# Expert-choice words of a cross-attention and mixture-of-experts kernel: turned by VectorE in squares of 32 and sent by four DMAs, so that the row comes back by column

## The reference, cut to what matters

```
x = x + xattn(layernorm(x), ctx)                       # 16 heads of 8
t = rmsnorm(layernorm(x)) * norm_w                     # [tokens, 128]
topw, topi = top_k(softmax(t @ gate_w.T), 2)           # 2 of 8 experts
h1 = t @ w1.T + 2 * (t @ a1[e].T) @ b1[e].T            # per chosen expert e, 512 wide
h3 = t @ w3.T + 2 * (t @ a3[e].T) @ b3[e].T
act = silu(h1) * h3
out = sum over the two e of weight_e * (act @ w2.T + 2 * (act @ a2[e].T) @ b2[e].T)
x = x + out
```

## Time and profile before

| | |
|---|---|
| time, median of 3 runs | 298.48 us (297.51 to 298.67) |
| time of the profiled execution | 297.54 us, span 295.8 us |
| TensorE busy | 285.6 us, 97% of the span |
| VectorE busy | 224.1 us, 76% |
| ScalarE busy | 187.6 us, 63% |
| GpSimd busy | 180.8 us, 61% |
| granted TensorE clock | 0.999 |
| DMA | 12.45 MB, mean 42 GB/s |

### The profile page before, as it was taken

One profiled execution on the slowest core, in us unless ns is written; L12 is line 12 of the kernel. 1 busy time (PEld: TensorE's weight loads), 2 busy tenths in 40 slices (PEclk: granted clock), 3 DMA queues, 4 the chain that ended last, 5 costly groups with the idle time before them and its releaser, 6 DMA issues. The chain is left out here.

```text
span 295.8 us, 4543 instructions
## 1 busy us (share of the span) xinstructions
PE 285.6 (97%) x1499; PEld 238.0 (80%) x1499; DVE 224.1 (76%) x610; ACT 187.6 (63%) x310; POOL 180.8 (61%) x183
## 2 busy tenths in 40 slices
PE   8779999999999999999999999999999999999995
PEld 6547788878888888888888888888888887878884
DVE  3878996986689658894589765895579965795694
ACT  2478967674945966757855868459656658555542
POOL 3376599198970889429990589608982389518400
PEclk9999999999999999999999999999999999999999
DMA  5720020100210021200221011200012000100001
GB/s 155 281 72 3 0 73 1 72 3 25 81 71 2 0 72 38 71 1 2 71 71 39 0 53 55 71 0 2 1 37 73 0 0 35 75 1 0 35 2 35
DMA packets 7225, 12.45 MB, mean 42 GB/s; under 512 B 1825, under 2 KB 3234, under 8 KB 7202
## 3 DMA queue, kind: packets, MB, share of 16 engines
q1 hardware_dynamic: 6768, 11.77, 11.5%
q10 hardware_dynamic: 434, 0.39, 0.4%
HBM read 10.03 MB, written 2.13 MB: 41 GB/s over the span
## 5 line engine op out<-in xcount | busy, mean ns | idle before, releaser
L1010 ACT ACTIVATE silu<-h_ps 128x512 f32<-128x512 f32 x64 | 37.5, 597 | 33.2 <-PE h_ps L642 31.7
L1681 POOL TENSOR_TENSOR um_lo<-umf,um_hi 128x1024 fp32r<-128x1024 f32 x7 | 16.9, 2409 | 60.4 <-ACT um_hi L1002 60.4
L642 PE MATMUL h_ps<-um_hi,b_hi 128*128 128x512 f32 x128 | 51.4, 401 | 0.0
L642 PE MATMUL h_ps<-um_lo,b_hi 128*128 128x512 f32 x128 | 50.3, 393 | 0.6 <-DVE um_lo L1330 0.6
L642 PE MATMUL h_ps<-um_hi,b_lo 128*128 128x512 f32 x128 | 49.9, 390 | 0.0
L1343 DVE TENSOR_TENSOR act_second<-silu,h_ps 128x512 f32<-128x512 f32 x32 | 21.7, 680 | 17.2 <-PE h_ps L642 15.3
L1343 DVE TENSOR_TENSOR act_first<-silu,h_ps 128x512 f32<-128x512 f32 x32 | 21.4, 680 | 15.9 <-ACT silu L1010 12.7
L1703 POOL TENSOR_TENSOR scaled<-act_second,ratio 128x512 f32<-128x512 f32 x23 | 29.8, 1297 | 1.3 <-DVE act_second L1343 1.3
L642 PEld LDWEIGHTS h_ps<-um_lo,b_hi 128*128 128x128 f32 x128 | 24.0, 188 | 7.1 <-DVE um_lo L1330 1.4
L1002 ACT CAST um_hi<-umf 128x1024 fp32r<-128x1024 f32 x14 | 14.8, 1054 | 23.2 <-DVE umf L1324 22.2
L642 PEld LDWEIGHTS h_ps<-um_hi,b_lo 128*128 128x128 f32 x128 | 24.1, 188 | 4.5
(11 more groups left out here) (294 smaller groups left out, 793.0 us busy)
## 6 DMA issues: line engine op xcount, KB each, us to landing
chosen<-choice_dram SPq DMA_DIRECT2D x7, 512.0 KB, 3.5
x_in<-in_x_dram SPq DMA_DIRECT2D x7, 256.0 KB, 2.9
ctx_in<-in_ctx_t_dram SPq DMA_DIRECT2D x7, 256.0 KB, 3.2
out_dram<-y SPq DMA_DIRECT2D x7, 256.0 KB, 2.0
act_second<-in_hidden_w_dram SPq DMA_DIRECT2D x1, 512.0 KB, 4.3
act_second<-in_lora_w_dram SPq DMA_DIRECT2D x1, 512.0 KB, 5.4
v_parts<-in_down_w_dram SPq DMA_DIRECT2D x1, 512.0 KB, 4.8
ctx_in<-in_ctx_t_dram ACTq DMA_DIRECT2D x2, 128.0 KB, 3.2
```

What stands on the lines that cost most here:

```text
L642: mm = nc.tensor.matmul((h1_ps, h3_ps)[s][n % 2][:], b13[w][:, s, c * P:(c + 1) * P], um[k][m][:, s, :], start=False, stop=(i == 2), skip_ ...
L1010: nc.scalar.activation(silu[:, n % SILU_RING, :], h1_ps[n % 2][:], ACT.Silu).then_inc(silu_done.sem, 1)
L1681: nc.gpsimd.tensor_tensor(um[1][1][:], umf[1][:], as_f32(um[1][0][:]), ALU.subtract)\
```

## The change

`choice` grows to 32 words for each token, of which eight are used; GpSimd clears it once at the start. A new VectorE instruction (`turn_choice`, one transpose of 128x32 in four squares of 32x32) turns it into `choice_t`, where partition 32a + c holds word c of the tokens 32a to 32a + 31. It stands in VectorE's program between `act_step(b, 5)` and `act_step(b, 6)` of every block but the last. SyncE then waits for this instruction and no longer for GpSimd's, and sends four DMAs of 8 partitions x 32 words in place of one of 128 partitions x 8 words. The row in DRAM and in `chosen` now runs over all tokens for word 0, then for word 1, and so on. The indices of the two choices now share a word, so the masks read bf16 elements 4 bytes apart and `ratio` reads its float32 elements next to each other. A pad of 8 words in SBUF is gone.

```diff
-        choice = sb("choice", [P, CHOICE])
-        chosen = sb("chosen", [P, P * CHOICE])
-
-        sb("spacer", [P, 8])
+        choice = sb("choice", [P, SQUARE])
+        choice_t = sb("choice_t", [P, SQUARE])
+        chosen = sb("chosen", [P, CHOICE * P])
...
         def chosen_index(k):
-            words = chosen[:].bitcast(BF16).rearrange("q (p c) -> q c p", c=2 * CHOICE)
-            return words[:, k * TILES:(k + 1) * TILES, :]
+            words = chosen[:].bitcast(BF16).rearrange("q (c p k) -> q c p k", c=CHOICE, k=TOP)
+            return words[:, 0:TILES, :, k]
 
         def chosen_gap():
-            return chosen[:].rearrange("q (p c) -> q c p", c=CHOICE)[:, INDICES // 2:, :]
+            return chosen[:, INDICES // 2 * P:]
...
             def spread_choice(n):
-                sp.wait_ge(choice_done.sem, choice_done.of(n))
-                sp.dma_start(choice_dram[n % 2].rearrange("(p c) -> p c", c=CHOICE), choice[:])\
-                    .then_inc(choice_out.sem, 16)
+                sp.wait_ge(choice_turned.sem, choice_turned.of(n))
+                rows_out = choice_dram[n % 2].rearrange("(c a p) -> a c p", c=CHOICE, p=SQUARE)
+                for a in range(P // SQUARE):
+                    sp.dma_start(rows_out[a], choice_t[a * SQUARE:a * SQUARE + CHOICE, :]).then_inc(choice_out.sem, 16)
                 sp.wait_ge(choice_out.sem, choice_out.of(n))
...
+            def turn_choice(n):
+                ve.wait_ge(choice_done.sem, choice_done.of(n))
+                if n > 1:
+                    ve.wait_ge(choice_out.sem, choice_out.of(n - 1))
+                nc.vector.transpose(choice_t[:], choice[:]).then_inc(choice_turned.sem, 1)
+
...
             act_step(0, 5)
+            turn_choice(1)
             first_weight(0)
             act_step(0, 6)
...
                 act_step(b, 5)
+                turn_choice(b + 1)
                 act_step(b, 6)
```

More of the change, by code:

```diff
@@ L45 @@
 CHOICE = INDICES // 2 + TILES
+SQUARE = 32
 WKV, A13, W13, B13, W2A2, B2 = range(6)
@@ L166, in build_program @@
         gap = sb("gap", [P, TILES])
-        choice = sb("choice", [P, CHOICE])
-        chosen = sb("chosen", [P, P * CHOICE])
-        sb("spacer", [P, 8])
-        choice_index, choice_gap = choice[:, 0:INDICES // 2].bitcast(BF16), choice[:, INDICES // 2:]
+        choice = sb("choice", [P, SQUARE])
+        choice_t = sb("choice_t", [P, SQUARE])
+        chosen = sb("chosen", [P, CHOICE * P])
+        choice_index, choice_gap = choice[:, 0:INDICES // 2].bitcast(BF16), choice[:, INDICES // 2:CHOICE]
         row_expert_sb = sb("row_expert_sb", [P, 1])
@@ L321, in build_program @@
         row_expert_in = sem("row_expert_in")
+        choice_clear = sem("choice_clear")
         choice_done = signal("choice_done", first=0)
-        choice_out = signal("choice_out", 16, first=0)
+        choice_turned = signal("choice_turned", first=0)
+        choice_out = signal("choice_out", 16 * (P // SQUARE), first=0)
         chosen_in = signal("chosen_in", 16, first=0)
@@ L997, in exp_ratio @@
                 sc.wait_ge(mask_scaled.sem, mask_scaled.of(n - 1))
-                nc.scalar.activation(tile4(ratio), chosen_gap(), ACT.Exp).then_inc(ratio_done.sem, 1)
+                nc.scalar.activation(ratio[:], chosen_gap(), ACT.Exp).then_inc(ratio_done.sem, 1)
             def um_high(n, k):
@@ L1669, in choice_words @@
                 pool.wait_ge(top_i_done.sem, top_i_done.of(n))
-                if n > 1:
-                    pool.wait_ge(choice_out.sem, choice_out.of(n - 1))
+                if n == 1:
+                    pool.wait_ge(choice_clear, 1)
+                else:
+                    pool.wait_ge(choice_turned.sem, choice_turned.of(n - 1))
                     pool.wait_ge(e_gap_done.sem, e_gap_done.of(n - 1))
@@ L1675, in choice_words @@
                 pool.wait_ge(gap_done.sem, gap_done.of(n))
-                nc.gpsimd.tensor_copy(choice_index.rearrange("p (k t) -> p t k", k=TOP), top_i[:, :, 0:TOP])\
+                nc.gpsimd.tensor_copy(choice_index.rearrange("p (t k) -> p t k", k=TOP), top_i[:, :, 0:TOP])\
                     .then_inc(choice_done.sem, 1)
@@ L1725, in _ @@
             nc.gpsimd.memset(minus_one[:], -1.0)
+            nc.gpsimd.memset(choice[:], 0.0).then_inc(choice_clear, 1)
             nc.gpsimd.memset(minus_half[:], -0.5).then_inc(const_pool, 1)
```

## The result

The changed kernel takes 304.12 us (median of 6 runs, 302.98 to 305.29) beside 297.97 us of the kernel before (6 runs, 296.87 to 298.67); the ratio is 1.0213, interval 1.019 to 1.0236. The forecast was 299.8 us with a range to 301.4. The profiled execution has a span of 302.8 us, 7.0 more than before.

A forecast was written before the change was run, and what follows sets the result against it. TensorE was busy 285.6 of 295.8 us, so only its waits counted: +2.53 (block 0) - 0.63 - 0.50 (turns into blocks 1 and 7) = +1.40 us; on the median 299.9, stated as 299.8 us, range 297.8 to 301.4.

The forecast's parts named there:

- the sum: Whole kernel: +2.53 in block 0, -0.63 and -0.50 at the turns into blocks 1 and 7, giving +1.40 us.
- Block 0: Den behind the transpose is held until GpSimd's z_lo ends, delaying ktv and TensorE's attention_out(2) by 2.53 us; bounds 0.5 to 2.7.
- The rival "not held": Block 0: den is not held, TensorE loses about 0.5 us, both waits go; -0.6, 297.9 us; chance 0.11.
- the restart of TensorE after 2.5 us: Block 0, TensorE after its stall: uncertain by some tenths, with the savings, within the forecast's own range of 299.2 to 300.5.
- The turns: TensorE's waits for um_lo at the turns into blocks 1 and 7 vanish, winning 0.63 + 0.50 = 1.13 us.
- nothing for the transpose in block 0: Block 0: the sum charges den's delay of 2.53 us but no separate cost for the transpose itself.
- The rival that the masks save nothing: VectorE's masks: stride is not what slows them, old waits remain and 2.53 come on top; 301.0 us; chance 0.08.
- I had given 0.1 and 0.49: VectorE's two masks: us saved on the first and the second by reading elements nearer each other.
- `ratio` halved as said: ScalarE's ratio: about half of its 1.24 us may go, but nothing is won as TensorE never waits behind it.
- The transposes and the DMAs: Blocks 1 to 6: transpose fits VectorE's idle time, words arrive about 0.5 us before the first mask; cost nothing.
- "held too": Every block: the transpose is also held beside GpSimd's z_lo, making the row late; 302.9 us; chance 0.12.
- "one behind the other": The four small DMAs run serially at 1.4 us each, 1.7 us lost in six turns; above 309 us; chance 0.03.

The follow-up runs named there:

- e2: Kernel before with the spacer behind chosen 56 words instead of 8, so tensors behind it lie 192 bytes higher; 301.81 us, ratio 1.0135.
- e3: Changed kernel with first_weight(0), which issues den, ahead of turn_choice(1) in block 0, addresses as in the changed kernel; 300.46 us, ratio 1.0109.
- e4: Changed kernel with den first in block 0 and every other tensor at its byte address of the kernel before; 297.20 us, ratio 0.9974.
- e15: Kernel before without the spacer behind chosen, so tensors behind it lie 32 bytes lower; 301.0 us, span 298.8 us.
- e1: Changed kernel with choice and choice_t at the end of SBUF and pads in their place, restoring all other old addresses; 298.68 us, ratio 1.005.
- e14: Kernel before with one more wait, VectorE waiting for GpSimd's words ahead of den in block 0, no transpose; 301.15 us, ratio 1.0109.
- e13: Changed kernel with den first and a 16-word pad behind chosen, so what follows lies 256 bytes above its old place; 297.09 us, ratio 0.9957.
- e9: Kernel before with a 48-word pad ahead of the first tensor, so every tensor lies 192 bytes higher; it cost nothing, total time not given.
- e11: Kernel before with the spacer 72 words, tensors behind chosen 256 bytes higher; as good as no move, total time not given.
- e10: Kernel before with only the weights 192 bytes higher and everything behind them 256 higher; matmul step 0.2295 us, total time not given.
- e7: Kernel before with um 192 bytes higher, z and b 256 higher; cost lay in the stage moved by 192, total time not given.
- e8: Kernel before with only the tensors from silu on 192 bytes higher; hidden steps kept their length, z and b's stage paid, total time not given.
- e16: Kernel before with the weights 224 bytes higher and everything behind them 256 higher; slow as well, total time not given.

## Why the prediction was wrong, step by step

**What failed: the sum has no term for the place of tensors in SBUF.** The part on the change says in words "A pad of 8 words in SBUF is gone", and the sum has nothing for it nor for the growth of `choice`. 3.6 (e2 against before) to 3.8 us (e3 against e4) are in it, more than every other term. The pad alone is worth 0.95% (e15: 301.0 us). Nothing in the trace of before could have priced it, but the diff showed allocations that change ahead of the tensors that TensorE streams, and a pad that no instruction uses.

**Block 0: right in mechanism and nearly in size.** `den` was held until GpSimd's `z_lo` was through (2.19 us forecast as 2.1), and `ktv` and TensorE's matmuls followed. With the addresses held, `attention_out(2)` comes 21.04 us behind the first `um_lo` matmul in e1 (52.91 - 31.87) and 21.05 in e14 (52.94 - 31.89), where it was 18.60 before: 2.44 us later, where the forecast had 2.53. The order alone, e1 against e4 with the transpose in both, is worth 2.3 us of span. The rival "not held" is refuted. By the rule of the Trainium skill that the prediction drew on (SBUF — State Buffer, Who interferes with whom), the trace agrees: the tensor_scalar waits, and the transposes, of which the seven take 203 to 212 ns each though GpSimd works beside them, do not.

**Missing: the clock behind the stall.** The range gave "the restart of TensorE after 2.5 us" and the savings some tenths together. It was 1.54 us in the profiled execution. It does not come every time (e1), so it adds nothing or about 1.5 us and widens the spread of the runs; the granted clock of the six runs lies between 0.983 and 0.994.

**The turns: right.** Both waits for `um_lo` are gone, in e1 and e13 too, where no fall of the clock keeps TensorE back. From `um_lo`'s matmul in block 0's first step to the same in block 7 the kernel before takes 265.28 - 32.20 = 233.08 us and e13 263.93 - 31.86 = 232.07, so 1.0 us is won, where the forecast had 1.13 and nothing for the transpose in block 0. The rival that the masks save nothing is refuted: 0.48 and 0.74 us beside 0.72 and 1.19, start to start 0.40 and 0.66 beside 0.63 and 1.09; I had given 0.1 and 0.49 and it is 0.23 and 0.43. `ratio` halved as said (617 ns).

**The transposes and the DMAs: right.** In block 2 the transpose lies in VectorE's idle time, and 0.58 us of it are left. The four issues took 1.30 us together, where the forecast had 0.47 from one to the next. The read back starts at 125.34 and lands after 3.6 us, at 128.9; the mask starts at 130.17 and waits for nothing. The rivals "held too" and "one behind the other" are refuted.

**The account.** From before to after in spans: -1.4 (e13's gain, of which about 0.3 are a quicker start whose cause is not known) + 2.3 (`den`) + 3.8 (addresses) + 1.5 (clock behind the stall) = 6.2 of the 7.0 us. Of the rest, some 0.5 stands at the start (the first `um_lo` matmul comes at 32.40 us, and at 31.86 in e13), where the granted clock is 0.74 between 15 and 20 us and was 1.00 before. This belongs to the execution and not to the change: the profiles of e9 and e11, which only move tensors, have 0.66 there as well. The runs of before that were taken beside e13's fall into two groups 1.2 us apart (297.1 to 297.4 us at 0.998 to 1.000, 298.1 to 298.9 at 0.993 and 0.994). With the addresses held (e1) and no fall of the clock, the forecast of +1.4 us would have met +0.9 of span.

## What to carry to other kernels

When a diff adds, drops or resizes an SBUF tensor, work out the addresses of what is allocated behind it before pricing an instruction: here the remainder modulo 256 between loaded weights and streamed tensors was worth 1.35% (e2), three times the change's own gain (0.43%). Put new small tensors at the end of the allocations, or pad by what restores the distance, and try the new kernel once with the old places. A tiny instruction like `den`, which took 2.19 and 2.33 us beside a large one of GpSimd and 0.16 ahead of it, must be issued ahead; a wait put in front of it can cost the length of the large one, and where TensorE stalls by it, the clock can add two thirds as much again (1.54 us behind 2.26).

## What the runs showed of the hardware that was not expected

- The distance between 128x512 float32 matmuls depends on where the streamed tensors lie relative to the weights: a mean of 0.2276 to 0.2279 us where that distance is a multiple of 256 bytes, 0.2315 to 0.2332 where it is another one throughout, except for 0.2295 in e10, all at a granted clock of 1.00. The Trainium skill (SBUF — State Buffer, Who interferes with whom) gives TensorE two independent read ports, one for the moving operand and one for the weights, and says that TensorE waits on nobody. By that no pad could change a step; the runs e2, e7, e8, e9 and e16 show that one does, and the measurement decides.
- After TensorE had been idle for 2.09 us in the changed kernel and 2.30 in e14, the granted clock went to 0.5, from 54.91 to 58.32 and from 52.79 to 56.20 us. After the same 2.30 us in e1 it did not.
- With bf16 elements 4 bytes apart in place of 32, the first mask (a tensor_scalar) took 0.48 us and not 0.72, and the second (a scalar_tensor_tensor) 0.74 and not 1.19.
